# A two-layer recurrent and attention network on one core: the recurrence's output product in high and low parts

## The reference

```python
xn = _layernorm(x)
Bu_re = einsum('btd,nd->btn', xn, gB_re)          # and Bu_im
new_re = A_re * h_re - A_im * h_im + bu_re        # scan over t, 32 complex states
new_im = A_re * h_im + A_im * h_re + bu_im
y = einsum('btn,dn->btd', H_re, C_re) - einsum('btn,dn->btd', H_im, C_im) + D * xn
g = silu(gelu(xn @ proj1.T + b1) @ proj2.T + b2)
x = x + y * g
```

## Time and profile before

| | |
|---|---|
| median of 3 runs | 819.32 us (818.69 to 820.13) |
| the profiled execution | 820.57 us |
| its span in the trace | 818.7 us |
| granted TensorE clock | 0.996 of full |
| TensorE busy | 800.7 us, 98% |
| VectorE busy | 666.7 us, 81% |
| ScalarE busy | 522.1 us, 64% |
| GpSimd busy | 468.0 us, 57% |

### The profile page before, as it was taken

How to read it: one execution, slowest core, us unless ns; L and a number is a source line. 1 busy time by engine, 2 the same in 40 slices (tenths; PEclk the granted TensorE clock), 3 DMA queues, 4 the chain that set the end, 5 groups by cost and what they waited for, 6 DMA issues and landing times.

```text
span 818.7 us, 22149 instructions
## 1 busy us (share of the span) xinstructions
PE 800.7 (98%) x7528; PEld 738.5 (90%) x7528; DVE 666.7 (81%) x2509; ACT 522.1 (64%) x1612; POOL 468.0 (57%) x1245
## 2 busy tenths in 40 slices
PE   7999999999999999999999999999999999999988
PEld 5988999888889899999999999999999999999967
DVE  6798787887687888988778887888888878897875
ACT  4554454454654787767767677677766767677582
POOL 6833022112335686676766667676676766667653
PEclk9999999999999999999999999999999999999999
DMA  8610012000001223221222312223221222212210
GB/s 303 232 34 1 1 65 66 1 1 1 1 14 33 55 45 59 49 53 35 45 48 51 62 33 47 40 45 59 45 53 35 45 49 51 59 33 48 41 40 28
DMA packets 101329, 41.09 MB, mean 50 GB/s; under 512 B 91744, under 2 KB 98400, under 8 KB 100576
## 3 DMA queue, kind: packets, MB, share of 16 engines
q1 hardware_dynamic: 98896, 38.89, 20.6%
q10 hardware_dynamic: 2320, 0.79, 0.4%
HBM read 14.47 MB, written 4.19 MB: 23 GB/s over the span
## 4 chain that ended last, share of the span: by engine, by line
PE 89%; DVE 4%; issue 2%; ACT 2%; POOL 2%; DMA 1%; ACTq 0%; POOLq 0%; DVEq 0%
PE bank L494 59%; PE bank L686 17%; PE bank L708 8%; PE bank L558 1%; POOL par L1727 1%; PE bank L568 1%; PE bank L608 1%; PE bank L511 1%; DVE QA L1492 1%; DVE PT L1526 1%; ACT SM L975 1%; DVE SM L1504 1%; PE bank L582 0%; DMA QT<-QA 0%; PE bank L633 0%
## 5 line engine op out<-in xcount | busy, mean ns | idle before, releaser
L1888 POOL TENSOR_SCALAR SM<-SM,stb 128x32 f32<-128x32 f32 (+7 forms) x512 | 195.1, 400 | 95.5 <-DVE stb L1511 91.9
L975 ACT ACTIVATE SM<-SM,stb 128x32 f32<-128x32 f32 (+7 forms) x512 | 206.1, 404 | 61.8 <-DVE stb L1504 58.1
L686 PE MATMUL bank<-KT,QT 128*128 128x192 f32 (+7 forms) x1024 | 166.9, 306 | 5.0 <-DVE stb L1504 4.8
L1504 DVE CUSTOM_DVE_ANT_0 SM<-bank,CONST 128x32 f32<-128x32 f32 (+7 forms) x512 | 126.7, 298 | 35.2 <-PE bank L686 32.4
L686 PEld LDWEIGHTS bank<-KT,QT 128*128 128x128 f32 x1024 | 147.0, 190 | 9.2 <-DVE stb L1504 5.9
L494 PE MATMUL bank<-yh,wq_lo 128*128 128x256 f32 x512 | 148.1, 289 | 0.2 <-DVE QA L1492 0.2
L494 PE MATMUL bank<-yl,wq_hi 128*128 128x256 f32 x512 | 144.2, 282 | 0.0
L494 PE MATMUL bank<-yh,wq_hi 128*128 128x256 f32 x512 | 144.1, 282 | 0.0
L1526 DVE STREAM_TRANSPOSE PT<-SM 128x384 f32<-128x384 f32 (+3 forms) x256 | 115.7, 481 | 18.6 <-PE bank L708 18.6
L494 PEld LDWEIGHTS bank<-yh,wq_lo 128*128 128x128 f32 x512 | 96.7, 189 | 0.4 <-DVE QA L1492 0.4
L494 PEld LDWEIGHTS bank<-yl,wq_hi 128*128 128x128 f32 x512 | 96.5, 189 | 0.0
(11 more groups left out here) (210 smaller groups left out, 1957.3 us busy)
## 6 DMA issues: line engine op xcount, KB each, us to landing
QT<-QA SPq DMA_DIRECT2D x248, 64.0 KB, 2.2
PT<-KV SPq DMA_DIRECT2D x256, 16.0 KB, 1.8
out<-fo SPq DMA_DIRECT2D x32, 128.0 KB, 2.0
X<-in_x SPq DMA_DIRECT2D x7, 512.0 KB, 11.6
stage<-in_wqn SPq DMA_DIRECT2D x2, 1024.0 KB, 9.7
stage<-in_wo SPq DMA_DIRECT2D x2, 1024.0 KB, 5.0
stage<-in_w1t SPq DMA_DIRECT2D x4, 256.0 KB, 5.7
stage<-in_w2t SPq DMA_DIRECT2D x2, 512.0 KB, 6.8
```

What stands on the lines that cost most here:

```text
L686: i = e.matmul(sbank[n % 2][:, at], Q[:, p, q, :, :].rearrange("p h c -> p (h c)"), KT[b % 3][:, p, 0:32 * q + 32], start=True, stop=True)
L975: i = e.activation(M[:, at], M[:, at], ACT.Exp, bias=S[:, 0, j:j + 1], scale=-1.0, accum_out=S[:, 1, j:j + 1])
L1504: i = e.tensor_tensor_reduce(M[:, at], bk[:, at], mask[:, 224 - 32 * q:256], 1.0, 3e38, ALU.add, ALU.min, S[:, 0, j:j + 1])
L1888: i = e.tensor_scalar(P[:, at], P[:, at], S[:, 2, j:j + 1], 1.0, ALU.mult, ALU.mult)
```

## The change

From chunk 1 on, `l0_y` calls `three` instead of the fp32 product: six fp32r products for two in fp32. For this the table and the states are split. ScalarE makes the high parts: `r_high` of RR at step 12, and `z_high(c, b)` at steps Z_AT = 14, 21, 29, 37, 45, 53, 61 for c = 1 to 7, b = 0 ahead of that step's gelu and b = 1 behind it. GpSimd makes the low parts: `r_low` at step 12 and both `z_low(c, b)` at the same steps, ahead of what else stands at that step and at later ones. The product y(1,0) and the states_out(1,0) that follows go from step 14 to step 15; all others keep their steps. Four tiles and their semaphores (rth, rtl, zth, ztl) are new.

```diff
+Z_AT = (14, 21, 29, 37, 45, 53, 61)
...
+        rh = sb("rh", [128, D], F32R, l0)
+        rl = sb("rl", [128, D], F32R, l0)
+        zh = [sb(f"zh{i}", [128, T], F32R, l0) for i in range(2)]
+        zl = [sb(f"zl{i}", [128, T], F32R, l0) for i in range(2)]
...
             def l0_y(c, b):
                 w.wait_ge("zz", 2 * c + b + 1)
                 w.wait_ge("sy", 2 * c + b)
+                if c:
+                    w.wait_ge("rth", 1)
+                    w.wait_ge("rtl", 1)
+                    w.wait_ge("zth", 2 * (c - 1) + b + 1)
+                    w.wait_ge("ztl", 2 * (c - 1) + b + 1)
                 for j in range(2):
-                    i = e.matmul(ubank[:, 256 * j:256 * j + 256], Z[b][:, 128 * j:128 * j + 128], RR[:, :],
-                                 start=True, stop=True)
+                    dst, sl = ubank[:, 256 * j:256 * j + 256], slice(128 * j, 128 * j + 128)
+                    if c:
+                        i = three(dst, zh[b][:, sl], zl[b][:, sl], rh[:, :], rl[:, :], True, True)
+                    else:
+                        i = e.matmul(dst, Z[b][:, sl], RR[:, :], start=True, stop=True)
                 i.then_inc(SEM["y"], 1)
...
-                if g in (10, 14, 22, 30, 38, 46, 54, 62):
-                    c = (10, 14, 22, 30, 38, 46, 54, 62).index(g)
+                if g in (10, 15, 22, 30, 38, 46, 54, 62):
+                    c = (10, 15, 22, 30, 38, 46, 54, 62).index(g)
                     l0_y(c, 0)
...
+            def r_high():
+                w.wait_ge("tab", 1)
+                e.activation(rh[:, :], RR[:, :], ACT.Copy).then_inc(SEM["rth"], 1)
+
+            def z_high(c, b):
+                w.wait_ge("zz", 2 * c + b + 1)
+                w.wait_ge("y", 2 * (c - 1) + b + 1)
+                e.activation(zh[b][:, :], Z[b][:, :], ACT.Copy).then_inc(SEM["zth"], 1)
...
+                if g == 12:
+                    r_high()
+                if g in Z_AT:
+                    z_high(1 + Z_AT.index(g), 0)
                 if g < 8 * NC:
                     l0_gelu(g)
+                if g in Z_AT:
+                    z_high(1 + Z_AT.index(g), 1)
...
-                if g in (10, 14, 22, 30, 38, 46, 54, 62):
-                    c = (10, 14, 22, 30, 38, 46, 54, 62).index(g)
+                if g in (10, 15, 22, 30, 38, 46, 54, 62):
+                    c = (10, 15, 22, 30, 38, 46, 54, 62).index(g)
                     states_out(c, 0)
...
+            def r_low():
+                w.wait_ge("tab", 1)
+                w.wait_ge("rth", 1)
+                e.tensor_tensor(rl[:, :], RR[:, :], rh[:, :].bitcast(F32), ALU.subtract).then_inc(SEM["rtl"], 1)
+
+            def z_low(c, b):
+                w.wait_ge("zth", 2 * (c - 1) + b + 1)
+                w.wait_ge("y", 2 * (c - 1) + b + 1)
+                e.tensor_tensor(zl[b][:, :], Z[b][:, :], zh[b][:, :].bitcast(F32),
+                                ALU.subtract).then_inc(SEM["ztl"], 1)
...
+                if g == 12:
+                    r_low()
+                if g in Z_AT:
+                    for half in range(2):
+                        z_low(1 + Z_AT.index(g), half)
                 if g == 48:
                     after_weights(w)
```

More of the change, by code:

```diff
@@ L63 @@
     "tx", "f1", "f2", "bu", "y", "wn_t", "wo_t", "ty", "mi_t", "tk", "tm", "q", "lo", "s", "pv", "o",
-    "w1h", "w2h", "bh", "xth", "gelu", "hsh", "sin", "th0", "wrh", "wnh", "wmh", "lbh", "woh",
+    "rth", "zth", "w1h", "w2h", "bh", "xth", "gelu", "hsh", "sin", "th0", "wrh", "wnh", "wmh", "lbh", "woh",
     "yth", "mi", "kt", "qn", "gx", "mt", "th1", "p", "oth",
@@ L70 @@
     "mx", "r", "qa", "pt", "otl", "ob",
-    "clean", "par", "ang", "nu", "tab", "rt", "fill", "rl", "lr", "kr", "kvr", "n", "qq", "nw", "rs", "oc", "kwk", "kwv",
+    "rtl", "ztl", "clean", "par", "ang", "nu", "tab", "rt", "fill", "rl", "lr", "kr", "kvr", "n", "qq", "nw", "rs", "oc", "kwk", "kwv",
 )
```

## The result

The changed kernel takes 824.65 us (median of 6 runs, 823.73 to 826.27) where the kernel before takes 819.34 us (6 runs): 5.3 us or 0.6% slower, ratio 1.0061 with a 95% interval of 1.0048 to 1.0073. Its profiled execution took 824.72 us with a span of 822.9 us.

The account below looks back on a forecast made before the run. The prediction took TensorE to bound the kernel (89% of the chain); its terms, 1.46 - 0.9 + 1.35 + 2.2 + 0.6 = +4.7 us, took the median from 819.32 to 824.0, range 820.6 to 826.8.

Parts of the forecast that it names:

- the likeliest case: Whole kernel: the engines' queues go as told, 824.0 us, from 821.8 to 826.3; chance 0.60.
- The product: l0_y in chunks 1 to 7: six fp32r products take 0.71 us for 0.86, saving 0.15 a call, 2.1 for 14.
- The prediction's other price, three passes of four: Each l0_y call at 0.65 us, fp32 counted as four passes; the sum 0.9 us lower over 14 calls; not adopted.
- The move: Chunk 1: y(1,0), hidden at step 14 before the wait for xl, stands on the path at step 15: +0.71 us.
- Chunk 4: Step 38: w_o(0,0) waits for GpSimd's weighing, queued behind z_low(4,*), until about 152.0; +1.35 us with y(4,1)'s saving.
- Chunk 6: Second layer's first turn: z_low(6,1) delays GpSimd's factors(0), so rs and l1_turn(0) come late: +2.2 us (1.2 to 3.3).
- Chunk 7: y(7,1) waits for VectorE, which two z_low collisions delay some 0.75 us; y(7,1) saves 0.15: +0.6 us.
- The table load: Chunk 7, ScalarE: gelu(61)'s table load falls behind z_high(7,0), gelu at 236.0 instead of 233.16; hidden by some 0.3 us.
- Chunk 1, the step that failed: Steps 14 and 15: +0.71 for the move, -0.15 for y(1,1), +0.9 for two collisions on VectorE; about +1.5 us.
- The rival in which one of the two stalls stays away: Chunks 4 and 6: one GpSimd stall does not come, 1.5 or 2.5 us less, 821.5 to 822.5; chance 0.17.
- the one with the table load: Chunk 7: the table load is not hidden, TensorE's last steps wait 1 to 2 us more, 825 to 826.5; chance 0.06.
- The rival on the other side: Faster, 817.2 us: 14 calls give all 2.1 if z_low(6,1) ends before 204.7, l1_turn(0) not kept; chance 0.05.

Follow-up runs that it names:

- best: The mended kernel with chunks 1 and 7 in fp32 as well, so only chunks 2 to 5 are split: 818.38 us, ratio 0.9983.
- no_splits: Changed kernel's products, y(1,0) at step 14, states split in chunk 1 only; chunks 2 to 7 multiply stale parts, output not the reference's: 818.93 us, ratio 0.9987.
- y_at_14: The changed kernel with y(1,0) and states_out(1,0) back at step 14, the splits kept: 825.03 us, ratio 1.0067.
- move_only: The kernel before with y(1,0) and states_out(1,0) at step 15, all products fp32, nothing split: 820.40 us, ratio 1.0008.
- left_weighing: The mended kernel with the weighing of step 37 behind z_low(4,*) on GpSimd again: 821.07 us, ratio 1.0020.
- mended: The changed kernel with y(1,0) at step 14, the weighing of step 37 ahead of z_low(4,*), and chunk 6 in fp32: 819.36 us, ratio 0.9991.
- left_chunk6: The mended kernel with chunk 6 split again and nothing else: 822.47 us, ratio 1.0043.
- c6_order: The changed kernel with z_low(6,1) behind factors(0) on GpSimd instead of ahead; every split and product stays: 824.13 us, ratio 1.0055.
- late_by_three: The kernel before with three added 128x512 sums on VectorE behind scan(1) of step 12, which nobody reads: 822.06 us, ratio 1.0031.

## Why the prediction was right, and where it was not

The time was forecast as 824.0 and came out at 824.65, in the likeliest case. By its steps:

- **The product.** Forecast 0.15 us a call; 0.16 in the traces of `best` (8 calls, 1.2 to 1.3 us). Right. The prediction's other price, three passes of four, would have given 0.21; the rows gave the better size. That chunk 6's share and y(7,0)'s are lost in waits is shown by `no_splits`.
- **The move.** Forecast +0.71 for a product that loses its cover. `y_at_14` against the changed kernel and `move_only` (0.87 with the fp32 product) show it.
- **Chunk 4.** Forecast +1.35 with a stall to about 152.0; TensorE started w_o at 151.98 and the chunk cost 1.4. `left_weighing` against `mended` shows it in the medians too. Right in mechanism and size.
- **Chunk 6.** Forecast +2.2 at the turn; measured +2.4 from step 55 to 56, with a wait of 2.67 us. rs came at 216.13 instead of 212.67, of which 1.0 was late already (2.83 in the table, less the 1.81 us by which up(12) was earlier in this execution). `left_chunk6` against `mended` shows it in the medians. Right. That the order alone is not the whole of it, `c6_order` shows: y(6,1) needs its low part at the same time as the turn needs rs.
- **Chunk 7.** Forecast +0.6, measured +0.97 at the second layer (`mended`, from step 58). Mis-sized: I gave VectorE 0.75 us for two collisions and it lost 1.0, in small operations that I had not counted. In the kernel before, the first row is 0.17 us long and the second 0.49 for its two. Most of this is not paid: at 260.66 `mended` is 0.67 us over `best`, of which 0.24 stood at step 58 already.

```profile
238.64 0.61 DVE L1473 TENSOR_TENSOR lg<-lg 128x16 f32<-128x16 f32 x1
...
241.09 1.04 DVE L1486 TENSOR_TENSOR ML<-ML,lg 128x128 f32<-128x128 f32 x2
```

- **The table load.** As forecast it fell behind z_high(7,0), and the lateness stayed covered:

```profile
237.75 0.42 ACT L896 ACTIVATE zh<-Z 128x256 fp32r<-128x256 f32 x1 [2.46 <-DVE Z L1344]
238.19 1.28 ACT L873 ACT_TABLE_LOAD   x1
239.49 0.69 ACT L873 ACTIVATE hs<-bank,B 128x512 f32<-128x512 f32 x1
```

- **Chunk 1, the step that failed.** Forecast +1.46, of it 0.9 for two collisions on VectorE; the trace has +2.5. The collisions cost 0.4: z_low(1,0) made h_low(12) 1.10 us long, and r_low cost VectorE nothing (rope_low 2.34 us, before 2.35). Missing from my sum was the clock: the move and the collision lengthened the wait from 0.79 to 2.07 us, and the lower clock behind it cost 1.5 us (`c6_order`, with the same wait and the clock at 1.00 behind it, has 1.11 at step 16 where the changed kernel has 2.64). I had asked what each wait costs and not what follows it.

- **The second layer.** The prediction put it at nothing ("Nothing after that adds or removes work; the second layer starts later by as much"). It starts 6.2 us later and gives 1.2 us back at 260.66, where the kernel before had a wait to lose.

So by the trace the change cost 5.06 us, and the sum had 4.7. The nearness is in part luck: 1.5 for the clock, 0.4 in chunk 7 and 0.2 in chunk 6 were too little, 0.5 for collisions and 1.2 in the second layer too much. The medians are 5.3 us apart, with an interval of 3.9 to 6.0. What separates one execution from another is not settled. Of the changed kernel's six runs the two with a mean clock of 0.998 took 823.7 and 824.0 us and the four with 0.996 took 824.6 to 826.3, but the kernel before, which has none of the new waits, spreads in the same way (in the first of the three sets 819.0 to 819.4 us at 1.000, 822.4 to 823.0 at 0.994). So the mean clock of a run does not tell whether it had the low stretch at step 14, and how often that comes behind which wait is open: a profile shows one execution. The Trainium skill ("TensorE: Matmul & The Clock Gate", Part 1) says that the array falls to 1.2 GHz when it has stood idle. The trace agrees that it falls; how long a wait it took here is told below. I should have weighed it for a wait that I forecast at over 2 us.

The rival in which one of the two stalls stays away was wrong, as was the one with the table load. The rival on the other side failed at its named point: z_low(6,1) ended at 209.35, not before 204.7.

## What to carry to other kernels

An instruction that waits in a strict queue delays all that stands behind it, so cost a split by what is queued behind its wait, and put ready work first; here the subtractions of two chunks, on a GpSimd that was idle for most of this layer, cost TensorE 1.6 and 2.4 us, twice what fourteen cheaper products could give. Before moving a product, ask whether it was covered where it stood. Where TensorE is the bound, keep its waits short: behind most of those of 1.8 us and more, another 1.0 to 1.5 us were paid here. And when two traces are laid on each other, follow the difference past the stage that was changed: a later wait can take part of it back.

## What the runs showed of the hardware

**The lower clock behind a wait.** From 30 us to the end of the span, the 14 profiles have eleven stretches of some 4 us at a low granted clock, each behind a wait of TensorE. By the length of the wait: 1.81 us, one of one; 2.07 and 2.08, three of four; 2.61, one of one; 2.66 to 2.68, three of four; 1.52 to 1.66, three of 22 (`move_only` at 277.71, `left_chunk6` at 785.61, `c6_order` at 788.28); 0.8 to 1.43, none of 33. So one and the same wait can bring it or not, and no sharp limit shows. Where the price could be told apart it was 1.0 to 1.6 us. `late_by_three` shows that a longer wait suffices, with no split. Low stretches in the first 25 us of the span, in most of the profiles, the kernel before included, are not counted.

**GpSimd held up beside VectorE.** One subtraction of 128x256 took 3.48 us on GpSimd beside VectorE's rope_low and what followed it, where the same shape takes 0.74 to 1.27 us elsewhere:

```profile
L1880 POOL TENSOR_TENSOR rl<-RR,rh x1: 3476/3476/3476, 52.8 to 52.8; 128x256 fp32r<-128x256 f32 x1
...
L1885 POOL TENSOR_TENSOR zl<-Z,zh x14: 737/946/1272, 59.9 to 241.2; 128x256 fp32r<-128x256 f32 x14
```

VectorE lost nothing there. Elsewhere it is VectorE that is held up (h_low 1.10 instead of 0.69). I had priced every meeting the same for VectorE. There z_low(1,0) had started first, at 59.92, and h_low at 60.31. At the 3.48 us rope_low had started first (52.09, the subtraction 52.76), but VectorE's instructions of 54.35 and 54.95, which started behind the subtraction, were not held up either (0.68 us each). Whether unbroken VectorE work always holds GpSimd up for as long was not tried.
